# The last stage of a two-layer decoder: exponentials with queries on partitions, turned by TensorE, in place of turned scores

## What is computed

```python
# plain attention: 16 heads of 32
scores = einsum('bhqd,bhkd->bhqk', q, k) * HD ** (-0.5)
scores = where(causal, -1e9, scores)
a = softmax(scores, axis=-1)
ctx = einsum('bhqk,bhkd->bhqd', a, v)      # then @ w_o
# shared attention: the same with 16 query heads over one picked key/value head, no w_o
```

## Time and profile before

| | us |
|---|---|
| median of 3 runs | 2117.59 (2116.45 to 2120.7) |
| the profiled execution, its own time | 2113.92 |
| its span, first to last instruction | 2112.1 |

### The profile page before, as it was taken

One profiled execution on the slowest core, in us unless ns is written; L12 is line 12 of the kernel. 1 busy time (PEld: TensorE's weight loads), 2 busy tenths in 40 slices (PEclk: granted clock), 3 DMA queues, 4 the chain that ended last, 5 costly groups with the idle time before them and its releaser, 6 DMA issues. The chain is left out here.

```text
span 2112.1 us, 33102 instructions
## 1 busy us (share of the span) xinstructions
PE 2039.2 (97%) x13727; PEld 1217.8 (58%) x13727; DVE 1164.7 (55%) x1819; ACT 514.6 (24%) x791; POOL 604.7 (29%) x580
## 2 busy tenths in 40 slices
PE   7899999999999999999999999999999999999986
PEld 5444444334444557565656656767676767676754
DVE  3567777567777754122222426465656575746667
ACT  2445555440000131111111122122222222222211
POOL 2122222228999600111110313123232322221212
PEclk9999999999999999999999999999999999999998
DMA  5101111205111046422121502100010101010000
GB/s 163 47 1 56 56 56 46 88 31 215 44 44 44 26 167 252 149 66 65 65 65 60 193 13 101 51 31 21 8 54 1 61 1 41 1 31 1 31 11 21
DMA packets 66240, 130.85 MB, mean 62 GB/s; under 512 B 6480, under 2 KB 19920, under 8 KB 66096
## 3 DMA queue, kind: packets, MB, share of 16 engines
q1 hardware_dynamic: 45968, 77.49, 11.1%
q10 hardware_dynamic: 14448, 32.64, 4.3%
q0 software_dynamic: 5680, 18.62, 3.0%
HBM read 97.40 MB, written 41.81 MB: 66 GB/s over the span
## 5 line engine op out<-in xcount | busy, mean ns | idle before, releaser
L1033 PE MATMUL conv_conv<-kv,toep 128*128 128x512 f32 x576 | 247.6, 592 | 0.1
L1623 PE MATMUL moe_gu_ps<-gu,xT_tile 128*128 x608 | 192.4, 459 | 0.0
L1033 PEld LDWEIGHTS conv_conv<-kv,toep 128*128 128x128 f32 x576 | 109.4, 190 | 138.2 <-issue 129.6
L2381 POOL TENSOR_TENSOR tail_rstd_x<-tail_rstd_x,const_minus_half 128x2 f32<-128x2 f32 x31 | 21.8, 703 | 464.6 <-DVE tail_rstd_x L2686 464.6
L1067 POOL TENSOR_TENSOR kv<-vT,cT 128x512 f32<-128x512 f32 x128 | 147.1, 1172 | 17.3 <-PE conv_conv L1033 13.5
L1623 PEld LDWEIGHTS moe_gu_ps<-gu,xT_tile 128*128 128x128 f32 x608 | 112.3, 190 | 66.5 <-issue 17.8
L2726 DVE RECIPROCAL tail_inv<-tail_ring 128x256 f32<-128x256 f32 x63 | 110.6, 1756 | 71.5 <-PE tail_ring L1976 69.5
L2389 POOL TENSOR_SCALAR_AFFINE_SELECT tail_expT<-tail_expT 128x1024 f32<-128x1024 f32 x64 | 72.2, 1130 | 189.3 <-ACT tail_expT L2488 189.1
L594 POOL TENSOR_SCALAR_AFFINE_SELECT front_expT<-front_expT 128x2048 f32<-128x2048 f32 x32 | 64.2, 2005 | 197.3 <-ACT front_expT L649 197.3
L2712 DVE TENSOR_REDUCE tail_negtop<-tail_scores 128x4 f32<-128x1024 f32 x64 | 78.2, 1221 | 70.8 <-PE tail_scores L1927 70.7
L1604 POOL DMA_INDIRECT xg<-x_after,tokens x37 | 35.0, 945 | 282.1 <-PE moe_xT_ps L1618 254.9
(11 more groups left out here) (430 smaller groups left out, 3992.4 us busy)
## 6 DMA issues: line engine op xcount, KB each, us to landing
toep<-toeplitz SPq DMA_DIRECT2D x32, 320.0 KB, 2.9
y_slots<-moe_y ACTq DMA_DIRECT2D x39, 256.0 KB, 2.0
gu<-in_L_ffn_gate_up_proj SPq DMA_DIRECT2D x5, 1408.0 KB, 12.0
toeplitz<-filt_rows SPq DMA_DIRECT2D x8, 768.0 KB
front_e<-in_ctx SPq DMA_DIRECT2D x8, 512.0 KB, 4.7
toeplitz<-filt_rows SPq DMA_DIRECT2D x16, 256.0 KB
x_after<-x SPq DMA_DIRECT2D x8, 512.0 KB, 5.0
tail_x<-x_after SPq DMA_DIRECT2D x8, 512.0 KB, 3.8
```

Of the source, the lines that this page charges most:

```text
L1033: ins = pe.matmul(bank, toep[p][:, mat * P:(mat + 1) * P], kv[p][:, c].rearrange("p b j i -> p (b j i)"), start=n == 0, stop=n == len(PART ...
L1623: ins = pe.matmul(gu_ps[:, s % 2, h, 0:HID], (xT if s else mid.xT_first)[:, c, :], wgu[c][:, e, h * HID:(h + 1) * HID], start=c == 0, stop ...
```

## The change

For each unit TensorE no longer computes the scores twice. The exponentials are taken from `scores` itself, one head and one query block at a time, since each row of queries has its own maximum as bias; ScalarE's accumulator gives the row sums. The exponentials go to SBUF rows (`exp_rows`), are scaled by GpSimd with the reciprocal sums (plain attention only), turned block by block by TensorE into three `ring` banks, copied by ScalarE to `expT`, and weighed. In the shared attention the division is made after `shared_out`, on 128x512, by VectorE. `scores` is now held until the exponentials are done. `scoreT`, `shift`, `split_top`, `mix`, `causal` and the matmuls by ones go. All five lists are written in a new order.

```diff
+                def turn_probs(kind, b, c):
+                    if kind == "P":
+                        pe.wait_ge(scaled, 4 * b + c + 1)
+                    else:
+                        key = (kind, "S", b, c)
+                        pe.wait_ge(quads.drained_sem(key), quads.count(key))
+                    rows = rows_of(kind, b, c)
+                    for n, (lo, hi) in enumerate(PARTS):
+                        key = (kind, "X", b, c, n)
+                        bank = ring.claim(pe, key)
+                        for g in range(4):
+                            ins = pe.transpose(bank[:, g * P:(g + 1) * P], rows[:, g, lo:hi], consts["ident"][:])
+                        ins.then_inc(ring.filled_sem(key), 1)
...
-                    for g in range(4):
-                        ins = pe.matmul(bank[32 * g:32 * g + 32, S:2 * S].rearrange("p (n q) -> p n q", q=P), ones32[:],
-                                        e[:, 1:3, g] if last else e[:, 1:4:2, g], start=False, stop=not last, skip_group_check=True)
...
+                def scale(b, c):
+                    pool.wait_ge(inverted, 4 * b + c + 1)
+                    rows = rows_of("P", b, c)
+                    for t, lo, hi in ((1, 0, S), (0, S, 3 * P)):
+                        part = rows[:, :, lo:hi]
+                        by = shares["P"][:, t, heads_of(c)].unsqueeze(2).to_broadcast([P, 4, hi - lo])
+                        ins = pool.tensor_tensor(part, part, by, ALU.mult)
+                    ins.then_inc(scaled, 1)
...
                 def exps(kind, b, c):
-                    key = (kind, "T", b, c)
-                    quads = quads_of(kind, b, c)
-                    act.wait_ge(quads.filled_sem(key), quads.count(key))
-                    act.activation(exp_buf(kind, b, c)[:, 0:3].rearrange("p n g q -> p g n q"),
-                                   quads.tile(key)[:, :, 0:3 * P].rearrange("p g (n q) -> p g n q", q=P), ACT.Exp).then_inc(quads.drained_sem(key), 1)
+                    n = unit(kind, b, c)
+                    act.wait_ge(top_ready, n + 1)
+                    key = (kind, "S", b, c)
+                    src, dst = quads.tile(key), rows_of(kind, b, c)
+                    for t, lo, hi in ((1, 0, S), (0, S, 3 * P)):
+                        for g in range(4):
+                            h = 4 * c + g
+                            ins = act.activation(dst[:, g, lo:hi], src[:, g, lo:hi], ACT.Exp, bias=negtop[:, t, h:h + 1],
+                                                 accum_out=sums[kind][b % len(sums[kind])][:, t, h:h + 1])
+                    ins.then_inc(quads.drained_sem(key), 1)
+
+                def take_probs(kind, b, c):
+                    for n in range(3):
+                        take((kind, "X", b, c, n), turned_of(kind, b, c)[:, n].rearrange("p g q -> p (g q)"))
+
+                def take_mixed(kind, b, c):
+                    take((kind, "W", b, c), mixedT[:, c, :])
...
+                def invert(b, c):
+                    key = ("P", "S", b, c)
                     dve.wait_ge(quads.drained_sem(key), quads.count(key))
-
-                def split_top(kind, b):
-                    top = negtop[:].unsqueeze(2).to_broadcast([P, NT, 4, NG])
-                    link.after(dve.tensor_copy(split[:, :, :, 0, :], top))
-                    dve.tensor_tensor(split[:, :, :, 1, :], top, split[:, :, :, 0, :], ALU.subtract).then_inc(split_ready[kind], 1)
-
-                def mix(kind, b, c):
-                    bank = filled((kind, "W", b, c))
-                    link.after(dve.reciprocal(inv[c % 2][:], bank[:, S:2 * S]))
-                    dve.tensor_tensor(mixedT[:, c, :], bank[:, 0:S], inv[c % 2][:], ALU.mult).then_inc(ring.drained_sem((kind, "W", b, c)), 1)
+                    dve.reciprocal(shares["P"][:, :, heads_of(c)], sums["P"][0][:, :, heads_of(c)]).then_inc(inverted, 1)
...
+                def shared_rows(b, t):
+                    key = ("A", "o", b, t)
+                    by = shares["A"][:, t, :].unsqueeze(2).to_broadcast([P, NG, HD])
+                    dve.tensor_tensor(weighted[:].rearrange("p (h d) -> p h d", d=HD), filled(key).rearrange("p (h d) -> p h d", d=HD), by,
+                                      ALU.mult).then_inc(ring.drained_sem(key), 1)
+                    dve.wait_ge(ring.drained_sem(key), ring.count(key))
+                    return dve.tensor_tensor(buf("x6", b)[:, t, :], weighted[:], buf("x5", b)[:, t, :], ALU.add)
```

889 lines of the change are left out of this document (407 added, 482 removed).

## The result

| | before | after |
|---|---|---|
| median of the runs, us | 2117.82 (2116.45 to 2120.70, 4 runs) | 2148.12 (2147.85 to 2148.77, 4 runs) |
| ratio, 95% interval | | 1.0146 (1.0134 to 1.0158) |
| profiled execution: own time, span, us | 2113.92, 2112.1 | 2148.11, 2145.9 |
| granted clock, mean | 0.994 | 0.983 |

The kernel is slower by 30.3 us. I had said slower, 2131, with a range from 2106 to 2152: the sign and the range hold, the size is more than twice the 13 us that I gave. That it lies inside the range is luck: the upper end was drawn for the third rival, which is not what happened.

The account below looks back on a forecast made before the run. TensorE was taken to bound the rounds, chains of waits the end. Work -5.2, round waits +12.7, start +4.8, end -0.8 and clock +4.0 made +15.5 on 2113.9, 2129.4 us; as a median 2131, range 2106 to 2152.

Parts of the forecast that it names:

- the third rival: Small exponentials don't overlap their accumulator reads, 4.9 us a unit instead of 3.3; ScalarE bounds in places: 2152 us, chance 0.09.
- TensorE's work, -5.2: Outside the end: twelve transposes a unit, 1.40 us, replace turned scores and matmuls by ones, 1.46; maxima's turns go: -5.2 us.
- The chain of a unit: From score to transposes in each unit: exponentials 3.3 us, GpSimd's products 3.7; transposes can start 5.6 (shared) or 9.7 (plain) after.
- ScalarE: In the rounds it gains 29 us a round and is then half busy, near 50 us in 100: no bound.
- rival 5: The change does not do what it says, in the built order of transposes and activations; chance under 0.01.
- rival 2: Half covered: rounds at +1 us, end at 0, giving 2114 to 2121 us; chance 0.12.
- Waits in the rounds, +12.7: Rounds 3 to 7: uncovered waits at second products of v and q and before the gates, 2.5 us x 5.
- Start, +4.8: Rounds 0 to 2: six old waits go (-4.85), four new ones come (9.65 us): +4.8 us.
- End, -0.8: From batch 7's wo projection: 147 us against the old 147.8, including 7.0 us idle before the last gates: -0.8 us.
- Clock, +4: After the 7 us idle and in the thin last batch, more work at lower clock: +4 us (0 to +10).
- The fourth rival: Transposes don't count as busy for the clock gate; the last 45 us run at 1.2 GHz: 2141 us, chance 0.04.
- The first rival: The lists cover everything: only saved work and removed old waits are left, 2103 us; chance 0.18.

Follow-up runs that it names:

- run 3: Changed kernel with four of the twelve transposes issued twice in 40 of the 64 units (160 more): 2163.31 us.
- run 4: Changed kernel with two exponential activations a unit in place of eight, without row sums and the maxima of three heads in four: 2131.05 us.
- run 6: Changed kernel with a weigh between the first and second products of v and of q in rounds 3 to 7: 2139.97 us.
- run 1: Changed kernel with GpSimd's product of unit (P,1,3) ahead of the root for x3 of batch 2: 2138.45 us.
- runs 2, 10 and 12: In order, from the changed kernel: last batch's x5 copies before exponentials, 2135.13 us; five reorderings together, 2106.57; those plus identity transposes in the last three waits, 2107.33.
- run 8: Changed kernel with 60 transposes of the identity filling TensorE's wait before the last gates: 2145.19 us.

## Why the prediction was right and wrong, point by point

- **TensorE's work, -5.2**: right. A round's busy time fell from 109.1 to 108.11, -5.0 in five rounds for the -4.0 of their share; run 3 gives 0.107 a transpose. (The 2235 for 275 ns a transpose left out the other terms of the sum: with them it is 2129.4 + 121.6 = 2251. Run 3 rules both out.)
- **The chain of a unit**: right, a little too dear. Exponentials 3.2 for 3.3, products 2.9 for 3.7.
- **ScalarE**: right. 53.5 us in 110 for 50 in 100, and beside the path in the rounds (run 4). Rival 3 is out, by 3.18 us a unit where it had 4.9; rival 5 by the rows of twelve transposes; rival 2 by the +5.6 of the rounds and the +6.3 of the end.
- **Waits in the rounds, +12.7**: right in places, 10.5 in size. The second products' waits are those named, and a piece of work between takes them away (run 6). `score(A,1)` has no wait, as its margin of 0.4 said.
- **Start, +4.8**: the step that failed. "New: 2.3 for x4 of batch 0 ...; 2.5 for the copy of its turned rows ...; 2.9 at `turn_probs(P,1,2)` ...; 1.95 in round 2 before the gates." What was named was there, 7.6 us for 9.65. Missing were 9.19 at `turn_probs(P,1,3)` (the product behind a root on GpSimd, 9.7 us with the clock by run 1) and 2.55 + 2.70 + 0.62 at the second products, which I had gone through only for the rounds. The terms of the start name VectorE's and ScalarE's lists and no step of GpSimd's, though its product is in the chain of every plain unit. And I wrote that no idle time would be named after GpSimd's products "in the rounds", which holds; the start was not asked.
- **End, -0.8**: the 7.0 us were 7.16, the three waits in the last units 2.26, 1.43 and 2.17. A unit takes 6.75 us at full clock (2106.04 to 2112.79; forecast 6.7) and 7.65 and 8.4 behind it, as the clock falls.
- **Clock, +4**: the second term that failed, mis-sized: 11.0 for 4, and in one place of two. 5.5 us went in the start, where I had none, and 2.8 + 5.0 in the end, where the kernel before had lost some too: two windows of 5 us at 0.69 and 0.66, with 3.5 us of work in each, are 2.3. That the 5.0 go with the clock rests on runs 2, 10 and 12.
- **Sum**: 15.5 for 34.2 of spans. Start +18.7, rounds -3.1, end +3.1.
- The fourth rival, transposes that don't keep the clock up, did not show as a rule (run 8). The half-speed stretch at the end that it described did come, at 5 us for its 10, and not in every trace. The sign I gave for it, a clock under 0.9 over the last 45 us, was a poor one: it is 0.69 in the kernel after, but in the kernel before it is 0.85 already, with the last 8 us free of any work of TensorE.
- The first rival's number, 2103, is 2107 as a median, and the reordered kernel has 2106.6. That is in part luck: the saved work is real once the lists cover the waits, but its start keeps 8.6 us of waits where the rival had none, and its end is 4 us shorter where the rival had 0.8.

## What to carry to other kernels

A step that is moved to another engine must be followed through every queue that it joins, prologue and epilogue included: the loop lost 1.1 us a round, and 28.6 of the 34.2 us came from places that run once. Where one engine's list has a step of the new chain behind one that waits for a later stage (a product behind a root, a copy behind exponentials), swap them before judging the idea: five such reorderings of one or a few lines turned 1.5% slower into 0.5% faster. After an idle time of TensorE count the work behind it at the lower clock, too: 5.5 us of the start and 7.8 less the 2.3 of before in the end, 11 of the 34.
